# Stacked keys of a decoder layer: laid out by DMAs through memory instead of by TensorE and ScalarE

## The reference, cut to what matters

```python
x = x + self_attention(layernorm(x))            # keys and queries through a convolution; tau, delta per head
x = x + cross_attention(layernorm(x), ctx_1024) # keys and values from ctx, mask over keys
x = x + moe(layernorm(x))                       # 64 experts, top 8, and a shared one
# in both attentions, for each head h:
scores = einsum('bhqd,bhkd->bhqk', Q, K) / sqrt(8)
out = einsum('bhqk,bhkd->bhqd', softmax(scores), V)
```

## Time and profile before

| | us |
|---|---|
| median of 3 runs | 342.3 (338.91 to 342.77) |
| the profiled execution, its own time | 338.21 |
| its span | 336.3 |
| TensorE clock granted, mean | 0.980 |
| TensorE / VectorE / ScalarE / GpSimd busy | 299.2 / 285.0 / 219.5 / 173.0 |

### The profile page before, as it was taken

The page is one execution under the profiler, slowest core; times in us unless marked ns, Lnnn a source line. Parts: engine busy times, 40 slices in busy tenths (PEclk is TensorE's granted clock), DMA queues, the critical chain, the costliest instruction groups (busy, mean ns, idle before and its releaser), DMA issues.

```text
span 336.3 us, 6408 instructions
## 1 busy us (share of the span) xinstructions
PE 299.2 (89%) x1705; PEld 206.3 (61%) x1705; DVE 285.0 (85%) x579; ACT 219.5 (65%) x458; POOL 173.0 (51%) x247
## 2 busy tenths in 40 slices
PE   0799959999998999999938987988999899999995
PEld 0634745666665566556625855756778677777773
DVE  4997796788878886887978799999998798899994
ACT  1296727768974667467517975566777577677773
POOL 9440020000350085044076786577888588888883
PEclk9999997999999999999969999799999999999999
DMA  7700021111311111210004756446662666776621
GB/s 285 236 1 0 9 55 31 25 40 33 63 34 32 32 41 25 42 23 2 2 0 126 218 169 217 138 153 197 195 197 79 223 203 216 224 220 218 217 91 62
DMA packets 30889, 36.80 MB, mean 109 GB/s; under 512 B 5136, under 2 KB 22288, under 8 KB 30736
## 3 DMA queue, kind: packets, MB, share of 16 engines
q1 hardware_dynamic: 30864, 36.51, 36.2%
HBM read 31.77 MB, written 0.79 MB: 97 GB/s over the span
## 4 chain that ended last, share of the span: by engine, by line
PE 41%; DVE 18%; POOL 18%; issue 12%; ACT 5%; DMA 4%; SPq 0%; POOLq 0%; DVEq 0%; ACTq 0%
PE bank L390 30%; POOL qbd L1467 11%; POOL kst L1444 5%; DVE conv L1360 2%; DMA conv<-coefficient_rows 2%; DVE kst L1166 2%; PE bank L512 2%; PE bank L537 2%; DVE rawmax L1129 2%; DMA xres<-x 1%; DVE qbd L1145 1%; PE bank L524 1%; PE bank L772 1%; DVE vs L1369 1%; POOL xn L277 1%
## 5 line engine op out<-in xcount | busy, mean ns | idle before, releaser
L390 PE MATMUL bank<-khl,kst 128*128 128x512 f32 x396 | 108.6, 410 | 15.2 <-DVE kst L1166 9.2
L1467 POOL TENSOR_TENSOR qbd<-vs,qbd 128x512 fp32r<-128x512 f32 x65 | 84.1, 1294 | 33.8 <-ACT qbd L1008 33.8
L390 PEld LDWEIGHTS bank<-khl,kst 128*128 128x128 f32 x396 | 71.8, 192 | 42.6 <-DVE kst L1166 18.3
L977 ACT ACTIVATE bank<-bank 128x512 f32<-128x512 f32 x63 | 36.7, 582 | 37.6 <-PE bank L390 37.6
L1129 DVE TENSOR_REDUCE rawmax<-bank 128x4 f32<-128x512 f32 x64 | 43.0, 683 | 12.7 <-PE bank L390 11.7
L1360 DVE TENSOR_TENSOR conv<-bank,conv 128x512 f32<-128x512 f32 x61 | 41.7, 684 | 8.3 <-DMA conv<-coefficient_rows 4.7
L1166 DVE TENSOR_TENSOR kst<-ring,kst 128x256 fp32r<-128x256 f32 x63 | 48.7, 773 | 0.0
L1369 DVE TENSOR_TENSOR vs<-conv,bank 128x512 f32<-128x512 f32 x66 | 45.3, 687 | 3.3
L1008 ACT ACTIVATE qbd<-vs 128x512 fp32r<-128x512 f32 x66 | 41.0, 622 | 7.3 <-DVE vs L1369 7.3
L263 POOL TENSOR_SCALAR nwt<-mv 128x4 f32<-128x4 f32 x4 | 0.9, 228 | 76.6 <-DVE mv L1023 76.6
L1444 POOL TENSOR_TENSOR kst<-ring,kst 128x128 fp32r<-128x128 f32 x64 | 39.2, 612 | 0.2
(11 more groups left out here) (195 smaller groups left out, 501.3 us busy)
## 6 DMA issues: line engine op xcount, KB each, us to landing
conv<-coefficient_rows SPq DMA_DIRECT2D x122, 128.0 KB, 3.0
ring<-w SPq DMA_DIRECT2D x66, 192.0 KB, 2.9
kbd<-kst SPq DMA_DIRECT2D x60, 64.0 KB, 2.0
pa<-pack_a SPq DMA_DIRECT2D x1, 1140.0 KB, 6.5
xres<-x SPq DMA_DIRECT2D x1, 512.0 KB, 4.2
ctxs<-ctxT SPq DMA_DIRECT2D x1, 512.0 KB, 7.1
outT<-qc SPq DMA_DIRECT2D x2, 256.0 KB, 2.1
pb<-pack_b SPq DMA_DIRECT2D x1, 449.0 KB, 7.8
```

Source lines behind the costliest of these rows:

```text
L390: return pe.matmul(out, lhsT, rhs, start=start, stop=stop)
L977: act.activation(out, four(2 + p), ACT.Silu).then_inc(silu_done, 1)
L1467: pool.tensor_tensor(hlo[:, k % 4, :].rearrange("p (b t) -> p b t", b=4), hx[k % 4], hhi[:, k % 4, :].bitcast(F32).rearrange("p (b t) -> p ...
```

## The change

- The half of self keys that belongs to batches 4 to 7, and all cross keys, are no longer stacked by `pick` and ACT. SP writes `khl[n]` to a tensor in memory, `split_keys` (0.5 MB and 1 MB), and reads it back into the rows of `kst[n]`, eight partitions in each DMA: 12 DMAs of 64 KB and 12 of 128 KB.
- POOL, not DVE, now makes `key_rows` (three small additions), and fills `kst[n]` with them ahead of those DMAs: 2048 and 4096 elements in each partition. This stands behind its first memsets and ahead of its bias addition and mask.
- SP issues the first store ahead of its loop, stacks in front of the `kbd` copies of s = 2, 3, 5, 6 and 7, and waits for them at s = 4 and 8.
- LATER keeps 4 query groups and 2 halves of values, at other PLACES.
- In every step ACT copies three quadrants into `qbd` and DVE one.

```diff
+            def store_keys(n, first):
+                sp.wait_ge(khi_ready, 2 * n + 2)
+                sp.wait_ge(klo_ready, 2 * n + 2)
+                sp.dma_start(split_keys[n, :, :, P * first:T],
+                             khl[n][:, :, first:B, :]...).then_inc(keys_stored, 16)
+            def stack_keys(n, first, places):
+                rows = split_keys[n].rearrange("(g j d) a t -> j d a g t", g=G, j=J)
+                for at, a in places:
+                    for j in range(J):
+                        r0 = 32 * j + at
+                        sp.dma_start(kst[n][r0:r0 + DK, :, first:B, :]...,
+                                     rows[j, :, a, :, P * first:T]).then_inc(kst_loaded, 16)
+            PARTS = ((S_HI, 0), (S_MID, 0), (S_LO, 1))
+            store_keys(0, 4)
             sp.wait_ge(rows_ready, 3)
             for s in range(1, STEPS):
-                sp.wait_ge(kst_ready, G * (2 * n + b // 4 + 1))
+                if s == 1: sp.wait_ge(kst_ready, G)
+                if s == 2: (wait kst_filled 1, keys_stored 16) stack_keys(0, 4, PARTS[0:2])
+                if s == 3: stack_keys(0, 4, PARTS[2:3]); store_keys(1, 0)
+                if s == 4: sp.wait_ge(kst_loaded, 16 * 3 * J)
+                if s == 5: (wait kst_filled 2, keys_stored 32)
+                if 5 <= s < 8: stack_keys(1, 0, PARTS[s - 5:s - 4])
+                if s == 8: sp.wait_ge(kst_loaded, 32 * 3 * J)
                 wait(sp, scored, G * (s - 1))
                 (four DMAs kbd <- kst, as before)

-        PLACES = [(0, 0), (0, 1), (0, 2), (0, 3), (1, 0), (1, 1), (1, 2), (1, 3), (2, 0), (2, 1), (2, 3),
-                  (3, 0), (3, 1), (3, 3), (4, 0), (4, 3), (5, 0), (5, 3)]
+        LATER = [("q", 0, 1, g) for g in range(G)] + [("v", 1, 0, 0), ("v", 1, 1, 0)]
+        PLACES = [(0, 1), (0, 3), (1, 1), (1, 3), (2, 1), (3, 1)]

 ACT:  +            act.wait_ge(key_rows_ready, 1)       # ahead of the first stacked_keys
       -                for j in range(2):                # queries_with_max
       +                for j in range(J - 1):
 DVE:  -            dve.tensor_reduce(key_rows...)
       -                for j in range(2, J):             # queries_with_max
       +                for j in range(J - 1, J):

 POOL, behind its memsets and the wait for pack_a:
+            link(pool.tensor_tensor(two, diag[:, 0:2, :, :], diag[:, 2:4, :, :], ALU.add))
+            link(pool.tensor_tensor(one, two[:, 0, :, :], two[:, 1, :, :], ALU.add))
+            pool.tensor_tensor(key_rows[:, :], one[:, :, 0], one[:, :, 1], ALU.add).then_inc(key_rows_ready, 1)
+            pool.wait_ge(key_rows_ready, 1)
+            for n, first in ((0, 4), (1, 0)):
+                pool.tensor_copy(kst[n][:, :, first:B, :].rearrange("p g b t -> p g (b t)"),
+                                 key_rows[:, :].unsqueeze(2).broadcast_to([P, G, T - P * first])).then_inc(kst_filled, 1)
```

More of the change, by code:

```diff
@@ L68, in sem @@
             return ctx.enter_context(nc.semaphore(name))
+        split_keys = nc.dram_tensor("split_keys", (2, P, 2, T), F32, kind="Internal").ap()
         bank = [ctx.enter_context(nc.psum_tensor(f"bank{i}", [P, 512], F32)) for i in range(8)]
@@ L120, in decoder_layer @@
         key_rows = sb("key_rows", [P, G])
+        key_sum = sb("key_sum", [P, 6 * G])
         on = sb("on", [P, H, DK])
@@ L200, in decoder_layer @@
         kst_ready = sem("kst_ready")
+        key_rows_ready = sem("key_rows_ready")
+        kst_filled = sem("kst_filled")
+        keys_stored = sem("keys_stored")
+        kst_loaded = sem("kst_loaded")
         kbd_ready = [sem(f"kbd_ready{i}") for i in range(2)]
@@ L289, in wait @@
                 eng.wait_ge(signal, value)
-        LATER = [(what, 0, 1, g) for g in range(G) for what in "qk"] + [("k", 1, c, g) for c in range(2) for g in range(G)]
-        LATER[8:8], LATER[11:11] = [("v", 1, 0, 0)], [("v", 1, 1, 0)]
-        PLACES = [(0, 0), (0, 1), (0, 2), (0, 3), (1, 0), (1, 1), (1, 2), (1, 3), (2, 0), (2, 1), (2, 3),
-                  (3, 0), (3, 1), (3, 3), (4, 0), (4, 3), (5, 0), (5, 3)]
+        LATER = [("q", 0, 1, g) for g in range(G)] + [("v", 1, 0, 0), ("v", 1, 1, 0)]
+        PLACES = [(0, 1), (0, 3), (1, 1), (1, 3), (2, 1), (3, 1)]
         def loaded(it, k):
@@ L335, in _ @@
                 sp.dma_start(ring[:, pair, :, :], w3v[:, pair, :, :]).then_inc(ld_w[pair], 16)
+            def store_keys(n, first):
+                sp.wait_ge(khi_ready, 2 * n + 2)
+                sp.wait_ge(klo_ready, 2 * n + 2)
+                sp.dma_start(split_keys[n, :, :, P * first:T],
+                             khl[n][:, :, first:B, :].bitcast(F32).rearrange("p a b t -> p a (b t)")).then_inc(keys_stored, 16)
+            def stack_keys(n, first, places):
[3 more added lines that the diff above has]
+                        r0 = 32 * j + at
+                        sp.dma_start(kst[n][r0:r0 + DK, :, first:B, :].bitcast(F32).rearrange("p g b t -> p g (b t)"),
+                                     rows[j, :, a, :, P * first:T]).then_inc(kst_loaded, 16)
+            PARTS = ((S_HI, 0), (S_MID, 0), (S_LO, 1))
+            store_keys(0, 4)
             sp.wait_ge(rows_ready, 3)
@@ L340, in _ @@
                 n, b = s // B, s % B
-                sp.wait_ge(kst_ready, G * (2 * n + b // 4 + 1))
+                if s == 1:
+                    sp.wait_ge(kst_ready, G)
+                if s == 2:
+                    sp.wait_ge(kst_filled, 1)
+                    sp.wait_ge(keys_stored, 16)
+                    stack_keys(0, 4, PARTS[0:2])
+                if s == 3:
+                    stack_keys(0, 4, PARTS[2:3])
+                    store_keys(1, 0)
+                if s == 4:
+                    sp.wait_ge(kst_loaded, 16 * 3 * J)
+                if s == 5:
+                    sp.wait_ge(kst_filled, 2)
+                    sp.wait_ge(keys_stored, 32)
+                if 5 <= s < 8:
+                    stack_keys(1, 0, PARTS[s - 5:s - 4])
+                if s == 8:
+                    sp.wait_ge(kst_loaded, 32 * 3 * J)
                 wait(sp, scored, G * (s - 1))
@@ L477, in later_stack @@
                     pe.wait_ge(qlo_ready, 2)
-                    pe.wait_ge(klo_ready, 4)
                 else:
@@ L483, in later_stack @@
                     else:
-                        pe.wait_ge(qst_ready if what_ == "q" else kst_ready, G * (2 * n_ + c_) + g_ + 1)
+                        pe.wait_ge(qst_ready, G * c_ + g_ + 1)
                 if what == "v":
                     values(n, c, bank[7])
-                elif what == "q":
+                else:
                     stack(bank[7], 0, qhl, c, g, q_stacked)
-                else:
-                    stack(bank[7], 2, khl[n], c, g, k_stacked)
             def later(s, place):
@@ L567, in second_inputs @@
             def second_inputs(c):
-                pe.wait_ge(kst_ready, 4 * G)
+                pe.wait_ge(v_copied, 4)
                 pe.wait_ge(qst_ready, 2 * G + 2 * c)
@@ L855, in _ @@
                 high_keys(1, c, 1 + c, Bw("bk"))
+            act.wait_ge(key_rows_ready, 1)
             for g in range(G):
@@ L893, in queries_with_max @@
                 wait(act, scoredT, G * (s - 1))
-                for j in range(2):
+                for j in range(J - 1):
                     r = slice(32 * j, 32 * j + 32)
@@ L1063, in _ @@
             later_taps(1, "del1")
[L1065 to L1068, removed]
             for m, at in ((0, S_HI), (0, S_LO), (1, S_MID), (2, S_HI), (2, S_MID), (3, S_LO)):
@@ L1142, in queries_with_max @@
                 wait(dve, scoredT, G * (s - 1))
-                for j in range(2, J):
+                for j in range(J - 1, J):
                     r = slice(32 * j, 32 * j + 32)
@@ L1410, in _ @@
                 pool.memset(low[:, g, 0:g], 1.0).then_inc(ones_ready, 1)
+            link, steps = chain(pool, pool_step)
             pool.wait_ge(ld_a, 16)
+            pool.wait_ge(ones_ready, 3 + GE)
+            pool.wait_ge(rows_ready, 3)
+            diag = ident.rearrange("p (j m c) -> p j m c", j=J, c=2)[:, :, 0:G, :]
+            two = key_sum[:, 0:4 * G].rearrange("p (j m c) -> p j m c", j=2, c=2)
+            one = key_sum[:, 4 * G:6 * G].rearrange("p (m c) -> p m c", c=2)
+            link(pool.tensor_tensor(two, diag[:, 0:2, :, :], diag[:, 2:4, :, :], ALU.add))
[5 more added lines that the diff above has]
+                                 key_rows[:, :].unsqueeze(2).broadcast_to([P, G, T - P * first])).then_inc(kst_filled, 1)
+            pool.wait_ge(kst_filled, 2)
             add_bias(pool, A("bo"), 0, B, B)
@@ L1414, in _ @@
             pool.tensor_scalar(maskb[:, :, :], masku[:, :, :], MASKED, None, ALU.mult).then_inc(mask_ready, 1)
-            link, steps = chain(pool, pool_step)
             pool.wait_ge(delta_ready, 2)
```

2 lines of the change are left out of this document (removed).

## The result

The changed kernel takes 349.74 us (median of 4, 347.13 to 351.5), before on the same chip 340.62 (median of 4): ratio **1.0258**, 95% interval 1.0154 to 1.0363. The forecast of 345.5 us was on the right side and too low by 4.2; the time lies in its range. It stood on a median of 342.3 for the kernel before, which is 340.62 in this comparison, so 1.7 us of what it came near by is the base: as ratios, 1.009 was forecast and 1.0258 measured, 5.6 us apart. The profiled execution took 348.81 us, with a span of 347.0 against 336.3. (Disturbed executions are left out of every ratio, which can therefore differ a little from the quotient of two medians.)

A forecast was written before the change was run, and what follows sets the result against it. Self attention was taken as shared between ACT and DVE, cross attention as PE's. 338.2 + 5.3 - 3.5 + 1.4, transfers 0, gave 341.4 us, or 345.5 on the median's scale; range 339.5 to 358.

The forecast's parts named there:

- fills hold DVE: At the start, POOL's fills block DVE's small instructions, so the first L277 starts near 18.1, not 12.77: +5.3 us.
- steps 0 to 6, work: Self attention: key stacks removed, one quadrant moved from DVE to ACT; sum -3.5 us, bounds -1.5 and -5.5.
- transfers: Store and stacks in SP's queue: issuing and transfers taken as hidden, 0; the other end +40 us.
- steps 7 to 15: Cross attention: +0.4 each in steps 7 and 11, +0.6 in step 15; sum +1.4 us, bounds 0 and +4.
- L263 and L1136: Small DVE instructions that took 3.07 and 1.78 us, ending with POOL's; cited as evidence that fills would hold DVE.
- Rival 2: At the start, the fills don't hold DVE: 340 us; chance 0.14.
- the wait for the values at place 1: Steps 2 and 3: DVE stands about 1.3 us for later cross values; net gain only 0.2 us each.
- The run of POOL's normalising: Steps 5 and 6: unchanged run of 7.5 us hanging on step 5, so only 0.2 us is gained there.
- the threshold of 1.5: Self steps: everything is hidden while a 128 KB stack takes no more than 1.5 us.
- rival 1: Stacks bound by few partitions, kbd copies land behind them: 2.4 us a stack, 11 us, 356 to 357 us; chance 0.38.
- its 27: 27 us from issuing the stacks of s = 5 until kbd of s = 7 is wanted, to hide 12 stacks.

The follow-up runs named there:

- e11: Changed kernel, store writes the high part twice so each stack DMA writes 24 partitions with the right numbers; 340.82 us, ratio 0.9996.
- e3: Changed kernel with the copies of query quadrants back at two for ACT and two for DVE; 348.43 us, ratio 1.0265.
- e5: Kernel before the change with only POOL's three additions and both fills put in behind its first memsets; 345.66 us, ratio 1.0127.
- e1: Changed kernel with POOL's two fills moved behind its bias, its mask and the first low queries; 345.16 us, ratio 1.0094.
- e2: Changed kernel with the same stack bytes in DMAs of 24 partitions, stacking other numbers than the kernel needs; 344.89 us, ratio 1.0147.
- e7: Changed kernel with e2's 24-partition DMAs (other numbers stacked) and quadrants at two for ACT, two for DVE; 342.5 us, ratio 1.0018.
- e4: Changed kernel with the two halves of cross values back at place 0 of steps 2 and 3; 349.94 us, ratio 1.0298.
- e6: Changed kernel with its 12 large stack DMAs issued 2, 2, 2, 2 and 4 at a time instead of 4, 4, 4; 343.69 us, ratio 1.0058.
- e12: Changed kernel with e11's wide stacks, e1's late fills, e4's places, and three quadrants on ACT only in the self attention; 335.7 us, ratio 0.9842.

## Why the prediction was right or wrong

Offset at step 15 in the profiled executions, by the terms of the sum (the clean steps are those of e11, which has the same work on the engines and no wait for a transfer):

| term | forecast | measured | read from |
|---|---|---|---|
| fills hold DVE | +5.3 | +4.8 to +5.1 | first `xn`; step 0 of e3, e5, e11 |
| clock ahead of step 0 | none | +2.2 | after less e11 at step 0 |
| steps 0 to 6, work | -3.5 | -3.7 | e11 from step 0 to 7 |
| transfers | 0 | +6.6 | steps 0 to 6 of after less e11's |
| steps 7 to 15 | +1.4 | +0.5 | after and e11 alike |
| sum | +3.2 | +10.6 | |

**The start: right.** The rows that I took as proof, L263 and L1136 held for the length of a POOL instruction, told what two instructions with operands in `nwt` would do, to 0.5 us. They told it as rows, not by the rule that I put beside them: both have one input (TENSOR_SCALAR and CAST), and POOL's memset beside L263 reads nothing, so they don't bear on two inputs against an instruction that reads. What I left open, whether a POOL copy does what a memset does, is now shown: the two fills set the lengths 1.81 and 3.51, and e1 takes them away. Rival 2 fell. The rule of the Trainium skill that I cited, page "SBUF — State Buffer", section "Who interferes with whom", names a DVE instruction with two inputs there; the trace agrees for the two held ones (L276 and L273, two inputs in `nwt`), and e1 agrees from the other side, for its copies at 36 us read a `bank`, and were not held.

**The clock: not foreseen.** After, e2 and e7 stand 2.2 to 2.6 us later at step 0 than e3, e5 and e11, which have the same fills; their windows at 46:52 have 0.72 granted, those of the other three 1.00. e4 and e6, with the same fills again, have 0.57 there and stand at +8.12 and +8.17. Among these eight kernels the start is the later, the less clock was granted ahead of it. These spells come and go between kernels with the same work there; what decides where one falls stays open, and so does whether they explain the spread between executions of one kernel.

**Steps 0 to 6: the sum right, its parts not.** Clean steps are 5.6, 5.85, 7.6, 7.5, 5.2, 5.2 and 5.9, forecast 5.4, 6.1, 7.3, 7.3, 5.4 and, for steps 5 and 6 together, 11.6. Steps 2 and 3 gave nothing: the wait for the values at place 1 that I put at 1.3 us takes it all, and e4 and e12 show 1.4 and 1.5 us for it in a step. Steps 4 and 5 gave 0.7 each, and e7 shows that this is the moved quadrant and not the removed stacks. The run of POOL's normalising, by which I allowed steps 5 and 6 only 0.2, is as long as before and PE waits for its end (0.45 us in e11), but it begins 3.0 us behind step 5's L558 and no longer 3.7: DVE, with one quadrant less, comes to its statistics earlier. So it is DVE's relief that moved the step, and the error was to hang the run on the step and not on DVE.

**The transfers: the step that failed.** "I take it as hidden, 0, since a kbd copy moved its bytes within its issue." The bounds, 0.60 to 4.8 us for a stack of 128 KB, were right; the 0 within them was not. Where stacks move alone, one takes **2.4 us** (55 GB/s in 86:88, above), 0.9 over the threshold of 1.5, as rival 1 had it. Its price, 12 x 0.9 = 11 us, was too high by 4.4, for it added the time of the `kbd` copies to that of the stacks. The packets of 69.3:94.3 show the two side by side:

```profile
DMA packets 2106, 2.14 MB, mean 85 GB/s; under 512 B 269, under 2 KB 1781, under 8 KB 2103
```

322 of them are of 4 KB, 32 for a stack, and 1512 of 512 B, 128 for a copy: 10 stacks and nearly 12 copies in 25 us. The stacks alone fill that time (10 x 2.4 = 24). With the copies left out of the prediction's count, 12 x 2.4 and 2.5 of landing are 31.3 us against its 27, which leaves 4.3 (an estimate); the waits for `kbd` come to 4.2:

```profile
PE bank L427 <- DMA kbd<-kst: 4.2, 2, 3.8
```

(the waits' view: us in total, times, longest). The 6.6 us are steps 4 and 5, 4.5 and 2.2 longer than e11's, and 0.7 in step 1, less 0.7 that step 6 gives back and 0.1 in steps 0 and 2. In step 4 that is 0.7 more than the wait of 3.8, behind which TensorE comes back at 1.2 GHz. In step 5 the lower clock (0.66) is what TensorE shows, but the last copy for s = 7, issued at 89.8, landed only 11.1 us later, at 100.9, and `scores(7, 0)`, which needs it, began at 101.17 (landings of the three copies issued from 88.6 to 89.8, then TensorE's timeline):

```profile
DMA to landing us min/median/max: 3.6/10.9/11.1
...
101.17 0.47 PE L427 MATMUL bank<-kbd,qst 128*128 128x512 f32 x1
```

At full clock TensorE would have stood there near 99.0 (94.33 + 5.21, less the 0.53 from this matmul to L558) and waited some 1.9 us, an estimate. So the late transfers alone account for most of step 5, and what the clock costs there by itself is not shown.

My reason for 0 was a copy into 32 partitions, and it doesn't carry over to eight: e2 and e11 change the number of partitions in a DMA and the wait is gone, with the same or more bytes; e6 changes how many stand in a row, and it is nearly gone. What in a narrow DMA is slow stays open. The share of 0.51 in 86:88 would also fit half of the 16 DMA engines being at work, and e2 and e11 change the rows read in memory with the partitions written.

**Steps 7 to 15: over-sized.** Step 7 lost 0.3 and step 11 0.45, as forecast in kind (ACT's high queries start 2.34 us behind L558 in step 7, before 1.69). But step 10 gave 0.2 back, and the way from step 15's L558 to the first of L594 (L560 before) grew by 0.04 us and not by 0.6: in both kernels PE first waits 0.68 us for ACT's `khl`, and then for no quadrant.

```profile
167.24 1.11 PE L427 MATMUL bank<-pb,xnT 128*128 128x64 f32 x8 [0.68 <-ACT khl L938]
```

**Taken together** the forecast's sum is +3.2 and the measured one +10.6; rival 1, with a chance of 0.38 and 356 us, had the mechanism and the price of a stack, and a sum that was too high by 4.4 us. That the time fell inside the range is owed to that rival, for which the range was stretched, and not to the forecast's own terms. On the medians the change costs 9.1 us. Taken away from it one at a time, by ratio, the fills give 5.6 us (e1; put into the kernel before they cost 4.3, e5), and the narrow transfers with what follows them 3.8 (e2) or 8.9 (e11). What stays open is the share of the clock's spells in these numbers, and so why e11's median lies 1.5% under e2's, of which their profiles show 0.7 (2.5 us of start).

## What to carry to other kernels

When layout work is moved from engines to DMAs, price a transfer by the partitions that one DMA writes, not by its bytes alone, and look at what stands behind it in the same queue; storing a part twice so that one DMA could write 24 partitions turned 1.0258 into 0.9996. A fill on POOL goes where DVE reads banks, not where it runs small instructions on the critical path: there the eight-element ones took as long as the fill. And a wait of TensorE can cost more than its length when the clock comes back at its lower level: step 4 lost 4.5 us with a wait of 3.8.

## What the runs showed of the hardware that I had not expected

- The DMA engines' busy share says little of the rate: 0.51 at 55 GB/s with stacks of 8 partitions alone, 0.65 at 81 with copies of `kbd` among them, 0.78 at 182 with stacks of 24 (e11):

```profile
69.00:71.00 2.00, 2.00 (x23) 1.38 (x11) 0.64 (x4) 1.00 (x2) 0.00 (x0) 1.00 0.78 182
```

- An issue by SP isn't of one price (ns, min/median/max): a stack of 8 partitions 0.30 us in the median of the change, one of 24 partitions 0.38 in e11, a `kbd` copy 0.60:

```profile
L353 SPq DMA_DIRECT2D kst<-split_keys x24: 274/302/553, 48.6 to 85.1; - x24
...
L353 SPq DMA_DIRECT2D kst<-split_keys x16: 320/376/601, 48.0 to 81.7; - x16
```

- After the 3.81 us in which TensorE stood still it came back at 1.2 GHz: 0.50 was granted in 93:95 and in 95:97, and the matmul at 93.31 took 0.80 us, where one of the same line took 0.40 at 104.59.

```profile
93.00:95.00 2.00, 1.69 (x4) 1.40 (x5) 0.70 (x2) 0.00 (x1) 0.00 (x0) 0.50 0.48 57
95.00:97.00 2.00, 2.00 (x20) 1.15 (x19) 1.90 (x5) 1.76 (x3) 0.00 (x0) 0.50 0.53 79
```
